# A slot's scores for the maxima in one block, its turned scores in another, with one wait for two banks each

## The chip, the cores and the metric

The kernel runs on one core of a Trainium2 chip. The metric is the device time of one execution in microseconds (us). Before the change it is 510.05 us, the median of three runs (509.32 to 510.07).

## The reference

Two layers act on `x` of shape 16 x 128 x 256 (batch, token, channel). Layer 0 is a WKV recurrence over the 128 tokens and a gated feed-forward with 704 hidden units. Layer 1 is a cross-attention and a mixture of eight experts plus a shared expert. The change lies in the cross-attention alone:

```
q = Wq @ layernorm(x) + bq;  k = Wk @ ctx + bk;  v = Wv @ ctx + bv      # 128 x 256 each
dot  = einsum('bhdt,bhds->bhts', q, k) / sqrt(8)                        # 16 heads of 8 dims
mask = target_mask[..., None] * source_mask[..., None, :]
dot  = mask * dot - (1 - mask) * 1e6
amap = softmax(dot, axis=-1) * mask
out  = einsum('bhts,bhds->bhdt', amap, v)
```

Per batch that is 16 heads of 256 x 256 scores. Sixteen batches are computed one behind the other.

## The kernel before

The kernel is written engine by engine, with semaphores set and waited for by hand; what an engine does, it does in the order in which it is written. In the attention the scores of every head are computed twice on TensorE (PE).

**Scores for the maxima.** `score` (L1190) multiplies a stack of 60 rows (bf16 parts of q, k and the mask) into a 128 x 512 bank of PSUM: two matmuls, tt = 0 and 1, each 128 queries by 256 keys. VectorE (DVE) takes the maximum over the keys of each query straight from the bank (`dve_reduce`, L1325). It does so two batches ahead. The negative maxima are turned (`pe_mxT`, L1279), copied by ScalarE (ACT, L1355), split into parts on GpSimd (POOL) and brought by DMA into the stack, so that the second computation subtracts them.

**Turned scores.** `score_T` (L1205) computes the same head with keys as rows, again two matmuls into one bank. ACT takes the exponential of the bank (`act_exp`, L1374) and writes it to SBUF. Eight matmuls of 32 columns (`pe_pv`, L1291) multiply it with the values and a column of ones, two slots later.

**Halves.** Head 2p and head 2p+1 of the maxima lie in different halves of the 128 rows (0 to 59 and 64 to 123), and so do the two halves of the turned heads. Matmuls in different halves run beside each other: their starts in the trace are 0.003 us apart.

**Slots.** A batch has 8 slots. Slot p of batch b holds, on PE (`pe_both`): scores 2p and 2p+1 for the maxima of batch b+2, turned scores 2p and 2p+1 of batch b, then the value matmuls of slot p-2. In slot 1 the value matmuls (`between`) stand inside `pe_both`, because they end the previous batch, and ACT copies their result (`act_av`, L1381) between its two exponentials of slot 1. Other work of PE follows in certain slots: the transpose of maxima behind slot 0, the four transposes of the previous batch's values (`pe_yT`, L1300) behind slot 3, two more (`pe_yo`, L1307) behind slot 5, a query projection (L688) behind slot 6. DVE's slot holds two maxima, and behind them in slot 3 the reciprocal of the sums (L1333, which waits for the four transposes), in slot 4 two products (L1340), in slot 5 the addition to X (L1348). ACT's slot holds two exponentials, with L1355 behind slot 0, a copy to PARTS (L717) behind slots 2 and 4, and L707 behind slot 7.

**Banks.** Scores for maxima use three banks (`SBK3`), turned scores three others (`TBK3`). Score n uses bank n mod 3, but score 15 uses that of 13 (`THIRDS`, L1167). `last_use(n)` is the score before n that used the same bank: n-3 in general, 13 for 15, 12 of the batch before for 0, and 15 of the batch before for 1. A score waits until maxima `last_use(n)` are taken (`a_red`), a turned one until exponential `last_use(m)` is done (`a_exp`). This order `pe_both` runs in 14 turns, from 179 to 341 us of the span. The first two batches' scores for maxima are written ahead of that, by `pe_scores` (L1230), a pair of heads at a time: head 2p tt 0, head 2p+1 tt 0, head 2p tt 1, head 2p+1 tt 1.

In `pe_both` before, each half of a slot is a group of four matmuls:

```
score_bank(pe, *to_score, n)                # wait: bank of score n
score(pe, to_score[1], n, 0, to)
turned_bank(pe, *to_turn, i, st, half)      # wait: bank of the turned score
score_T(pe, to_turn[1], i, st, 2 * half)
score(pe, to_score[1], n, 1, to).then_inc(a_s, 1)
score_T(pe, to_turn[1], i, st, 2 * half + 1).then_inc(a_st, 1)
```

Of the kernel before, what the change touches and what calls it, by code (L numbers as in the profile page):

```python
# [14 lines left out]
NG, GB = 4, 4  # L15
# [3 lines left out]
HEADS, HD = 16, 8  # L19
# [31 lines left out]
def flamingo_kernel(nc, x, ctx, mask, g_xattn, g_ffn, time_decay, time_first, gate_wT, up_wT, down_wT,  # L51
# [11 lines left out]
    with ExitStack() as keep:  # L63
# [161 lines left out]
        with ExitStack() as part:  # L225
# [8 lines left out]
            def semp(name):  # L234
                return sem(name, part)
# [126 lines left out]
            def later(count):  # L362

                return not isinstance(count, int) or count > 0
# [762 lines left out]
            with ExitStack() as att:  # L1127
# [18 lines left out]
                a_mx = [semp(f"a_mx{k}") for k in range(NS)]  # L1146
# [4 lines left out]
                a_s = semp("a_s")  # L1151
                a_red = semp("a_red")
# [3 lines left out]
                a_st = semp("a_st")  # L1156
                a_exp = semp("a_exp")
# [9 lines left out]
                THIRDS = [n % 3 for n in range(HEADS - 1)] + [1]  # L1167
                SBK3, TBK3 = [bank[2], bank[0], bank[1]], bank[3:6]

                def last_use(n):  # L1170

                    return max(m for m in range(-HEADS, n) if THIRDS[m % HEADS] == THIRDS[n])
# [6 lines left out]
                def rows_of(h):  # L1179

                    lo = 64 * (h // HALF)
                    return slice(lo, lo + STACK), h % HALF

                def head_of(n):

                    return n // 2 + HALF * (n % 2)

                def score(pe, k, n, tt, to):
                    rows, h = rows_of(head_of(n))
                    return pe.matmul(to[:, tt * T:(tt + 1) * T], QKA[rows, k, 0, h, tt * P:(tt + 1) * P],  # L1190
                                     QKA[rows, k, 1, h, :], start=True, stop=True)
# [5 lines left out]
                def turned_head(q, m):  # L1197

                    return HALF * (m // 2) + 2 * column_of(q, m) + q % 2

                def score_T(pe, k, q, st, m, to=None):
                    rows, h = rows_of(turned_head(q, m))
                    if to is None:
                        to = TBK3[THIRDS[turned_at(q, st, m // 2)]]
                    return pe.matmul(to[:, (m % 2) * T:(m % 2 + 1) * T], QKA[rows, k, 1, h, st * P:(st + 1) * P],  # L1205
                                     QKA[rows, k, 0, h, :], start=True, stop=True)

                def turned_at(i, st, half):

                    return 2 * (2 * i + st) + 1 - half  # L1210

                def score_filled(pe, g, k, n):

                    if n == 0:
                        pe.wait_ge(a_qa[k], 32 * (g + 1))

                def score_bank(pe, g, k, n):

                    score_filled(pe, g, k, n)
                    pe.wait_ge(a_red, HEADS * (GB * g + k) + last_use(n) + 1)  # L1220

                def turned_bank(pe, g, k, i, st, half):

                    b, m = GB * g + k, turned_at(i, st, half)
                    if m == 0:
                        pe.wait_ge(a_mx[k], 32 * (g + 1))
                    if later(HEADS * b + last_use(m) + 1):
                        pe.wait_ge(a_exp, HEADS * b + last_use(m) + 1)
# [31 lines left out]
                def pe_both(pe, to_score, to_turn, p, between):  # L1260


                    i, st = p // 2, p % 2
                    for n, half in ((2 * p, 1), (2 * p + 1, 0)):
                        to = SBK3[THIRDS[n]]
                        if first(GB * to_turn[0] + to_turn[1]) and n in (1, 2):
                            pe.wait_ge(s_x2, 1 + 2 * G3 + n)
                        score_bank(pe, *to_score, n)
                        score(pe, to_score[1], n, 0, to)
                        turned_bank(pe, *to_turn, i, st, half)  # L1270
                        score_T(pe, to_turn[1], i, st, 2 * half)
                        score(pe, to_score[1], n, 1, to).then_inc(a_s, 1)
                        score_T(pe, to_turn[1], i, st, 2 * half + 1).then_inc(a_st, 1)
                        if half == 1:
                            between()

                def pe_mxT(pe, g, k):
                    pe.wait_ge(a_red, HEADS * (GB * g + k + 1))
# [180 lines left out]
                def first(b):  # L1459

                    return isinstance(b, int) and b == 0
# [35 lines left out]
                with nc.Block() as block:  # L1497
# [143 lines left out]
                    def _(pe):  # L1641
# [41 lines left out]
                        def slot(_, g, k, p):  # L1683
# [14 lines left out]
                            if there(b, AHEAD_S):  # L1698
                                pe_both(pe, at(g, k, AHEAD_S), (g, k), p, values if p == 1 else nothing)
                            elif there(b):  # L1700
                                pe_scoresT(pe, g, k, i, st)
# [597 lines left out]
```

## Time and profile before

| | |
|---|---|
| median of three runs | 510.05 us |
| the profiled execution | 509.36 us |
| its span, first to last instruction | 507.6 us |
| granted TensorE clock, mean | 0.997 |
| PE busy in the span | 474.1 us (93%) |
| DVE busy | 381.3 us (75%) |
| ACT busy | 244.9 us (48%) |
| POOL busy | 230.1 us (45%) |

The span runs from the first instruction to the last; the execution's time is 1.8 us more. Matmuls are pipelined and overlap, so "busy" of PE says that some matmul was under way, not that the array worked at its peak. A mean of 273 ns for a score matmul is its latency; the next one in the same half starts 0.11 to 0.12 us later. The time an engine sat idle ahead of a group is written behind the group, with the instruction that released it.

### The profile page before, as it was taken

The numbers are of one execution on the slowest core, as the hardware profiler recorded it, in microseconds if no ns is written. First come the engines' busy times: TensorE is split into PE (matmuls) and PEld (weight loads), VectorE is DVE, ScalarE is ACT, GpSimd is POOL, SyncE is SP. The second block draws the span as 40 slices with busy tenths as digits, with TensorE's granted clock in tenths as the row PEclk, the third lists the DMA queues.
The fourth block names the chain that finished last, engine by engine and source line by source line (L and its number), as shares of the span: only waits on it lengthen the run. The fifth ranks groups of instructions, "written<-read, shape, count | busy, mean of one in ns | idle before, by whom it ended". The sixth has DMA issues, their size and how long they took to land. (4 is left out here: it accounts for less than half of the span.)

```text
span 507.6 us, 10286 instructions
## 1 busy us (share of the span) xinstructions
PE 474.1 (93%) x3384; PEld 259.3 (51%) x3384; DVE 381.3 (75%) x765; ACT 244.9 (48%) x461; POOL 230.1 (45%) x319
## 2 busy tenths in 40 slices
PE   2998999998999999999999998998999999999993
PEld 2663664854733633343343333333445647788882
DVE  4989889899888789999999999998465633333321
ACT  2761232332232078889999998787412010233331
POOL 3736434154755355867677763213010660042433
PEclk9999999999999999999999999999999999999998
DMA  7750175002775116566566655300022224378843
GB/s 237 216 176 0 43 166 89 2 0 62 186 195 150 54 57 174 147 171 184 162 163 172 171 153 147 84 5 5 1 94 77 74 94 166 120 185 195 192 112 41
DMA packets 67256, 59.96 MB, mean 118 GB/s; under 512 B 10048, under 2 KB 62256, under 8 KB 67216
## 3 DMA queue, kind: packets, MB, share of 16 engines
q1 hardware_dynamic: 63712, 55.24, 39.6%
q0 software_dynamic: 3072, 4.21, 4.9%
q8 instruction: 22, 0.36, 0.3%
q14 instruction: 18, 0.15, 0.1%
q10 hardware_dynamic: 432, 0.00, 0.0%
HBM read 38.90 MB, written 22.50 MB: 121 GB/s over the span
## 5 line engine op out<-in xcount | busy, mean ns | idle before, releaser
L1325 DVE TENSOR_REDUCE MX<-psum 128x2 f32<-128x512 f32 x256 | 162.1, 682 | 10.0 <-PE psum L1190 8.4
L1374 ACT ACTIVATE HP<-psum 128x512 f32<-128x512 f32 x224 | 122.1, 602 | 28.9 <-PE psum L1205 26.4
L1190 PE MATMUL psum<-QKA 60*128 60x256 bf16 x512 | 81.3, 273 | 7.1 <-DVE MX L1325 5.6
L1205 PE MATMUL psum<-QKA 60*128 60x256 bf16 x512 | 81.1, 273 | 1.5 <-DMA QKA<-max_scr 1.0
L1291 PE MATMUL psum<-HP,VP 128*32 128x256 f32 x1024 | 81.8, 391 | 0.3 <-issue 0.2
L602 PE MATMUL psum<-space_a,space_w 128*128 128x512 f32 x160 | 73.1, 602 | 1.9 <-DVE HP L629 1.9
L1190 PEld LDWEIGHTS psum<-QKA 60*128 60x128 bf16 x512 | 31.6, 94 | 63.8 <-DVE MX L1325 44.6
L1966 POOL DMA_INDIRECT out_x<-OE,to_u x16 | 24.9, 1557 | 62.6 <-ACT OE L2001 60.1
L602 PEld LDWEIGHTS psum<-space_a,space_w 128*128 128x128 f32 x160 | 29.0, 190 | 36.5 <-issue 31.0
L2089 PE MATMUL psum<-XT,WE 128*128 128x256 f32 (+1 forms) x192 | 44.0, 379 | 0.9 <-ACT XT L1985 0.9
L199 PE MATMUL psum<-space_a,wsh 128*128 128x512 f32 (+1 forms) x96 | 43.6, 598 | 0.3 <-PEq L1497 0.3
L615 ACT ACTIVATE space_a<-psum,hgs 128x512 f32<-128x512 f32 (+1 forms) x24 | 15.6, 649 | 54.8 <-PE psum L602 49.5
L2089 PEld LDWEIGHTS psum<-XT,WE 128*128 128x128 f32 (+1 forms) x192 | 34.3, 181 | 7.3 <-issue 1.1
L1291 PEld LDWEIGHTS psum<-HP,VP 128*32 128x32 f32 x1024 | 20.6, 108 | 28.8 <-issue 18.1
L1205 PEld LDWEIGHTS psum<-QKA 60*128 60x128 bf16 x512 | 30.6, 94 | 6.9 <-issue 3.6
L2250 DVE SCALAR_TENSOR_TENSOR KR<-KR,psum 128x256 f32<-128x256 f32 (+1 forms) x24 | 10.1, 420 | 30.0 <-ACT KR L1992 30.0
L1413 POOL TENSOR_TENSOR NP<-NM,zeros 32x128 bf16<-32x128 f32 x32 | 14.3, 446 | 36.6 <-ACT NM L1355 35.3
L644 PE MATMUL psum<-space_w,HP 128*128 128x256 f32 x120 | 27.3, 381 | 0.9 <-PEq L795 0.9
L199 PEld LDWEIGHTS psum<-space_a,wsh 128*128 128x128 f32 (+1 forms) x96 | 16.6, 181 | 21.2 <-issue 21.1
L739 POOL TENSOR_TENSOR QK<-QK,PARTS 128x512 f32<-128x512 f32 x16 | 18.5, 1157 | 18.9 <-ACT PARTS L717 18.8
L489 DVE RECIPROCAL DEN<-DEN 128x256 f32<-128x256 f32 (+1 forms) x12 | 27.0, 2264 | 0.0
L1992 ACT ACTIVATE KR<-psum 128x256 f32<-128x256 f32 (+1 forms) x24 | 9.2, 382 | 36.9 <-PE psum L2089 36.9
(207 smaller groups left out, 767.3 us busy)
## 6 DMA issues: line engine op xcount, KB each, us to landing
QKA<-stack_scr SPq DMA_DIRECT2D x32, 480.0 KB, 4.5
stack_scr<-PARTS SPq DMA_DIRECT2D x32, 192.0 KB, 2.1
WE<-in_W SPq DMA_DIRECT2D x16, 352.0 KB, 4.0
stack_scr<-PARTS SPq DMA_DIRECT2D x32, 128.0 KB, 2.0
XD<-dispatched SPq DMA_DIRECT2D x8, 258.0 KB, 3.9
X<-in_x SPq DMA_DIRECT2D x4, 512.0 KB, 5.8
CTX<-in_ctx SPq DMA_DIRECT2D x4, 512.0 KB, 8.2
MB<-in_mask SPq DMA_DIRECT2D x16, 128.0 KB, 3.3
```

What stands on the lines that cost most here:

```text
L199: last = pe.matmul(bank[2 * i + side][0:m, :], (wsh1, wsh3)[side][:, h, i * P:i * P + m], ZT4[:, h, bass.ds(GT * g, GT)], start=(h == 0), ...
L489: dve.reciprocal(DEN[:, h, x], DEN[:, h, x]).then_inc(s_rec, 1)
L602: last = pe.matmul(to[:, :], w[:, h, i * P:(i + 1) * P], ZT[:, h, :], start=(h == 0), stop=(h == 1))
L644: pe.matmul(to[f], HP[:, i, t * P:(t + 1) * P], dw[:, i, :], start=(i == 0), stop=False)
L739: pool.tensor_tensor(QK2 if r == 0 else part_of(2), QK2, part_of(r), ALU.subtract).then_inc(a_rest, 1)
L1190: return pe.matmul(to[:, tt * T:(tt + 1) * T], QKA[rows, k, 0, h, tt * P:(tt + 1) * P], QKA[rows, k, 1, h, :], start=True, stop=True)
L1205: return pe.matmul(to[:, (m % 2) * T:(m % 2 + 1) * T], QKA[rows, k, 1, h, st * P:(st + 1) * P], QKA[rows, k, 0, h, :], start=True, stop=True)
L1291: last = pe.matmul(PVB[32 * j:32 * j + 32, (m // 2) * T:(m // 2 + 1) * T], VP[:, k, st, turned_head(i, m), :], PT[:, i % 2, st, m, :], sta ...
L1325: dve.tensor_reduce(MX[:, par, head_of(n), :], src[:, :].rearrange("p (a s) -> p a s", a=2), axis=AX.X, op=ALU.max).then_inc(a_red, 1)
L1374: act.activation(PT[:, i % 2, st, 2 * half:2 * half + 2, :].rearrange("p j t -> p (j t)"), TBK3[THIRDS[m]], ACT.Exp).then_inc(a_exp, 1)
L1966: pool.indirect_dma_start(out=out_rows, out_offset=bass.IndirectOffsetOnAxis(ap=to_u[:, e, a:a + 1], axis=0), in_=OE[:, s, a, :], in_offse ...
L2089: last = pe.matmul(bank[i][0:m, lo:lo + CAP], w[:, s, h, i * P:i * P + m], XT[:, s, h, :], start=(h == 0), stop=(h == 1))
```

## The change

In each slot of `pe_both`, the four matmuls of the two scores for the maxima come first, then (in slot 1) the value matmuls, then the four turned ones. Ahead of the first block stands one wait for the maxima of `last_use(2p+1)`, ahead of the second one wait for the exponential of `last_use` of the slot's second turned score. The matmuls are the same in number, operands and banks. A score's semaphore is still raised by its second matmul.

```
-                    for n, half in ((2 * p, 1), (2 * p + 1, 0)):
-                        to = SBK3[THIRDS[n]]
+                    for n in (2 * p, 2 * p + 1):
                         if first(GB * to_turn[0] + to_turn[1]) and n in (1, 2):
                             pe.wait_ge(s_x2, 1 + 2 * G3 + n)
-                        score_bank(pe, *to_score, n)
-                        score(pe, to_score[1], n, 0, to)
-                        turned_bank(pe, *to_turn, i, st, half)
-                        score_T(pe, to_turn[1], i, st, 2 * half)
-                        score(pe, to_score[1], n, 1, to).then_inc(a_s, 1)
-                        score_T(pe, to_turn[1], i, st, 2 * half + 1).then_inc(a_st, 1)
-                        if half == 1:
-                            between()
+                        score_filled(pe, *to_score, n)
+                    pe.wait_ge(a_red, HEADS * (GB * to_score[0] + to_score[1]) + last_use(2 * p + 1) + 1)
+                    for tt in range(2):
+                        for n in (2 * p, 2 * p + 1):
+                            last = score(pe, to_score[1], n, tt, SBK3[THIRDS[n]])
+                            if tt == 1:
+                                last.then_inc(a_s, 1)
+                    between()
+                    if p == 0:
+                        pe.wait_ge(a_mx[to_turn[1]], 32 * (to_turn[0] + 1))
+                    b, m = GB * to_turn[0] + to_turn[1], turned_at(i, st, 0)
+                    if later(HEADS * b + last_use(m) + 1):
+                        pe.wait_ge(a_exp, HEADS * b + last_use(m) + 1)
+                    for j in range(2):
+                        for half in (1, 0):
+                            last = score_T(pe, to_turn[1], i, st, 2 * half + j)
+                            if j == 1:
+                                last.then_inc(a_st, 1)
```

## Rows read from the trace of the kernel before

**Rows 1.** The 14 turns: busy us of PE, PEld, DVE, ACT, POOL; clock, DMA.
```profile
180.30:341.20 160.90, 154.46 (x1879) 60.40 (x1879) 153.92 (x285) 142.14 (x283) 95.62 (x158) 1.00 0.53 141
```

**Rows 2.** Groups from 210 to 300 us: busy, mean ns | idle before, releaser.
```profile
L1325 DVE TENSOR_REDUCE MX<-psum 128x2 f32<-128x512 f32 x125 | 79.5, 683 | 4.0 <-PE psum L1190 3.1
L1374 ACT ACTIVATE HP<-psum 128x512 f32<-128x512 f32 x124 | 67.5, 602 | 8.9 <-PE psum L1205 7.4
```

**Rows 3.** Timeline of DVE: start us, us, instruction, count, idle before it.
```profile
235.00 3.95 DVE L1325 TENSOR_REDUCE MX<-psum 128x2 f32<-128x512 f32 x6
239.15 0.69 DVE L1325 TENSOR_REDUCE MX<-psum 128x2 f32<-128x512 f32 x1 [0.20 <-PE psum L1190]
240.04 3.08 DVE L1325 TENSOR_REDUCE MX<-psum 128x2 f32<-128x512 f32 x5 [0.20 <-PE psum L1190]
243.04 0.34 DVE L1333 RECIPROCAL RD<-psum 128x32 f32<-128x32 f32 x1
243.31 1.28 DVE L1325 TENSOR_REDUCE MX<-psum 128x2 f32<-128x512 f32 x2
244.50 0.60 DVE L1340 SCALAR_TENSOR_TENSOR YA<-psum,maskG,RD 128x128 f32<-128x128 f32 x2
245.02 1.28 DVE L1325 TENSOR_REDUCE MX<-psum 128x2 f32<-128x512 f32 x2
246.21 0.41 DVE L1348 TENSOR_TENSOR X<-X,psum 128x256 f32 x1
246.54 3.94 DVE L1325 TENSOR_REDUCE MX<-psum 128x2 f32<-128x512 f32 x6
...
248.42 0.68 DVE L1325 TENSOR_REDUCE MX<-psum 128x2 f32<-128x512 f32 x1
```

**Rows 4.** Timeline of ACT in the same batch.
```profile
239.26 0.60 ACT L1374 ACTIVATE HP<-psum 128x512 f32<-128x512 f32 x1 [0.17 <-PE psum L1205]
239.75 0.59 ACT L1381 ACTIVATE AV<-psum 128x512 f32<-128x512 f32 x1
...
240.72 0.60 ACT L1374 ACTIVATE HP<-psum 128x512 f32<-128x512 f32 x1
241.67 0.65 ACT L717 ACTIVATE PARTS<-QK 128x512 bf16<-128x512 f32 x1
242.19 2.30 ACT L1374 ACTIVATE HP<-psum 128x512 f32<-128x512 f32 x4
```

**Rows 5.** Timeline of PE in the same batch.
```profile
238.50 0.28 PE L1279 MATMUL psum<-ident,MX 128*32 128x128 f32 x1
238.72 0.28 PE L1190 MATMUL psum<-QKA 60*128 60x256 bf16 x1
238.72 0.28 PE L1205 MATMUL psum<-QKA 60*128 60x256 bf16 x1
...
239.04 0.64 PE L1291 MATMUL psum<-HP,VP 128*32 128x256 f32 x8
239.62 0.28 PE L1190 MATMUL psum<-QKA 60*128 60x256 bf16 x1
...
239.85 0.27 PE L1190 MATMUL psum<-QKA 60*128 60x256 bf16 x1
...
241.39 0.28 PE L1205 MATMUL psum<-QKA 60*128 60x256 bf16 x1
...
242.28 0.66 PE L1300 MATMUL psum<-ident,AV 128*128 128x128 f32 x4
242.87 0.28 PE L1190 MATMUL psum<-QKA 60*128 60x256 bf16 x1
...
249.16 0.28 PE L1190 MATMUL psum<-QKA 60*128 60x256 bf16 x1
```

**Rows 6.** Timelines of PE and DVE in the prologue, around one pair.
```profile
165.07 0.39 PE L1190 MATMUL psum<-QKA 60*128 60x256 bf16 x4 [0.79 <-DVE MX L1325]
165.48 0.69 DVE L1325 TENSOR_REDUCE MX<-psum 128x2 f32<-128x512 f32 x1
```

## The prediction

> **What bounds the kernel now.** I read the share of busy time first. Over the 160.90 us in which both kinds of scores are written, PE is busy for 154.46 us, DVE for 153.92 and ACT for 142.14 [rows 1]. No engine is far from full, so any wait that the change puts between two of them has little room to vanish in. The groups of instructions show who waits: in 90 us DVE waits 4.0 us ahead of 125 maxima and ACT 8.9 us ahead of 124 exponentials, nearly all of it for PE [rows 2]. 125 maxima in 90 us are 11.52 us for a batch of 16. The timeline of DVE shows the same period (the batch's third last pair starts at 235.00 and at 246.54, 11.54 us apart) and where the waits stand: 0.20 us ahead of the maxima of score 2 (239.15) and of score 3 (240.04), and about 0.2 us ahead of score 0, inside the merged line at 235.00 [rows 3]. Last I read the chain PE -> DVE -> PE for its latencies, since the change only moves matmuls and waits: it removes no instruction that computes.
>
> **Constants, each read from a row.** Within a batch I count from the first score matmul, S0 = 0. S, T, V are the starts of a slot's score matmuls, turned-score matmuls and value matmuls; R(n) and E(n) the starts of reduction n and exponential n.
> - Reductions back to back: (3.08 - 0.68) / 4 = 0.60 apart. The reciprocal adds 0.27 (243.04 to 243.31), the two products 0.52 (244.50 to 245.02), the addition to X 0.33 (246.21 to 246.54) [rows 3].
> - A bank given back: the reduction at 248.42 ends 0.68 later, at 249.10, and the score that needs the bank starts at 249.16 [rows 3, 5]. So S >= R(n) + 0.74.
> - Scores to reduction: S at 238.72, R at 239.15: 0.43 [rows 3, 5]. Four matmuls of two heads written as a pair stand in the prologue already: 0.39 us from first start to last end, then R at 165.48, 0.41 after the start [rows 6]. So a pair costs no more time than one head did, because the heads of a pair lie in different halves of the rows, and R(2p) >= S + 0.43.
> - Turned scores to exponential: T 238.72, E 239.26: 0.54. Exponentials are 0.49 apart (239.26 to 239.75), the copy AV takes 0.49, a PARTS copy 0.52 (241.67 to 242.19) [rows 4, 5].
> - Turned bank given back: E at 240.72 ends 0.60 later, T starts at 241.39. So T >= E(n) + 0.67 [rows 4, 5]; I use 0.66.
> - PE in order: S to V 0.32 (238.72 to 239.04), V to the next 0.58 (239.04 to 239.62; I use 0.57), two matmul pairs 0.23 (239.62 to 239.85), the transpose of the maxima 0.22 (238.50 to 238.72), the four of AV 0.59 (242.28 to 242.87) [rows 5].
>
> **What the change does to each slot.** A slot now waits once, for the later of the banks of its two scores, writes the four score matmuls, waits once for the later of the two turned banks, and writes the four turned ones. The same matmuls overlap two by two as before, so the matmul time is unchanged at zero difference (0.39 us for four shows it [rows 6]). Each slot has two waits on PE fewer. No row prices a wait that is already met; two such steps stand inside the 0.23 us from 239.62 to 239.85, two matmul pairs that take 2 x 0.11 [rows 5], so they are worth between 0 and 0.01 us, and I take 0. What remains is what each wait holds back.
>
> *Middle slots (p = 1 to 6)* wait for the maxima of score 2p-2: R(2p) >= R(2p-2) + 0.74 + 0.43 = 1.17, against two reductions, 1.20. It fits with 0.03 to spare, if PE is there on time.
> *Slots 7 and 0.* Score 15 has the bank of 13, and score 1 of the next batch the bank of 15. Now score 14 waits for maxima 13 and score 0 for maxima 15, the one just ahead. R(14) - R(13) and R(0) - R(15) become 1.17 instead of 0.60: 0.57 of idle DVE twice, where now about 0.06 and 0.2 stand.
> *Slot 1.* The value matmuls (between) stand between the scores and both turned scores. That is good for the reductions: R(2) = S1 + 0.43 and R(3) follows 0.60 later, so the waits of 0.20 there go. But T1 comes after V, 0.9 us later than S1, and what is queued behind it on ACT is the exponential, then AV, then the other exponential.
>
> Walk through one batch: S0 0, R0 0.43, R1 1.03, T0 0.22, E0 0.76, E1 1.25, V 0.54, maxima's transpose 1.11 (0.57 after V), S1 1.33, R2 1.76, R3 2.36. V of slot 1 at 1.65, T1 2.22, E2 2.76, AV 3.25, E3 3.74. S2 = R2 + 0.74 = 2.50, R4 2.96, R5 3.56. T2 needs E2's bank: 2.76 + 0.66 = 3.42 (without that wait it would be 2.73). V 3.74, S3 4.31: R6 is 4.74, where DVE was ready at 4.16, 0.58 lost. E4 4.23, T3 = 4.23 + 0.66 = 4.89, V 5.21, the transposes of AV 5.78, S4 6.37. The reciprocal waits for those transposes (0.66 long, plus 0.04): 6.48, where R7 + 0.60 = 5.94: 0.54 lost again. R8 = S4 + 0.43 = 6.80. From here DVE leads: S5 7.54; R9 7.40, the products 8.00, R10 8.52, R11 9.12, addition 9.72, R12 10.05, R13 10.65, S7 = 11.39, R14 11.82, R15 12.42, and S0 of the next batch at 13.16. ACT is ready for it: E15 = T7 + 0.54 + 0.49 = 12.64, its bank is free at 13.30, T0 would start at 13.38.
>
> The period is 13.16 us. In check: 16 x 0.60 = 9.60, operations between 1.12, waits 0.57 + 0.57 + 0.13 (R2) + 0.58 + 0.54 + 0.05 (R8) = 2.44.
>
> **The sum.** 14 turns run in this order. The first has no AV, transposes of values or reciprocal behind it; the walk without them gives about 11.3. Twelve take 13.16, and the last, up to the end of its reduction 15, 12.42 - 0.43 + 0.68 = 12.67. Together 11.3 + 157.9 + 12.7 = 181.9, against 160.9 [rows 1]: +21.0 us. The profiled execution took 509.36 us (span 507.6), 0.14% below the median of 510.05; 509.36 + 21.0 = 530.4, and I say 530.5. Nothing before or behind this stretch is changed, and the stretch ends on PE and DVE together, so its delay reaches the end in full.
>
> What no row shows is how ACT behaves once the turned scores wait for its exponentials in pairs. Low bound: T2 and T3 cost nothing, and only slots 7 and 0 and R2 count: 9.60 + 1.12 + 0.57 + 0.57 + 0.13 = 11.99, 0.47 above 11.52, some 14 x 0.47 = +6.6, 516. High bound: the loss of slot 3 occurs once more, in slot 4 (0.4 a batch, +5.6), 536. The rows stand nearest to the walk, whose waits of T are all longer than 0.3 us past what PE would reach by itself.
>
> The Trainium skill, "TensorE: Matmul & The Clock Gate", Part 3, "The cost: per-tile semaphore tail", says that increments which concurrent matmuls make on completion serialise, about 26 ns each. The change puts two such increments side by side. The prologue's pair has them side by side too, and its reduction starts 0.02 us after the pair's last modelled end, against 0.03 to 0.04 with one head [rows 3, 5, 6]: the trace does not show the cost. By the rule, an estimate with 26 ns in each of the five places where a pair leads straight into a wait is 0.13 a batch, 1.8 us, 532.
>
> **The rivals.**
> (a) *ACT's wait is hidden, only the ends of a batch cost*: 516, as worked out. For it: ACT has 18.8 us of idle in the stretch [rows 1]. Against it: that idle is 1.3 us a batch, and the order exp, AV, exp in slot 1 cannot use it before E2.
> (b) *Faster.* The reductions 2 and 3 lose their waits of 0.20 each in the middle of the batch [rows 3], and the waits at the batch's ends cost nothing. Price: 0.4 x 14 = 5.6 us, 504. It decides if a bank comes back early enough, within 0.60 - 0.43 = 0.17 us of the start of a reduction, or if PE is so late at slots 7 and 0 anyway that the wait is over. The rows have 0.74 for the first, and for the second only 0.2 of lateness.
> (c) *No change*: the gain of (b) and some 0.4 a batch at the ends cancel: 510. It needs T2 hidden as well.
> (d) *Worse*: ACT's lateness is not recovered by slot 5 but carried into the next batch, 0.5 to 1 us more a batch: 537 to 545. For it: ACT has 1.3 us of slack a batch and the walk takes most of it in slots 1 to 4. Against it: in slots 5 to 7 the walk has PE wait for DVE, not ACT.
>
> **How the numbers follow.** Forecast 0.76, with its own range 524 to 535; (a) 0.10; (d) 0.08; (b) 0.03; (c) 0.03. What can be told from no change here is about 0.2%. Slower is the forecast, (a) and (d), 0.94; same is (c), 0.03; faster (b), 0.03. The range for 8 times in 10 is 520 to 536.
>
> **What would show it.** In the trace after: a period of about 13.2 us; DVE idle of 0.5 to 0.6 us ahead of maxima 14, 0 and 6 and ahead of the reciprocal, none ahead of maxima 3; the turned scores of slot 2 about 0.9 us after its scores, not with them; PE waiting for ACT where now it waits for DVE alone. Wrong would be: a period under 12.2 (then ACT's wait was hidden), turned scores of slot 2 right behind their scores, or reductions 14 and 0 at 0.60 from the ones ahead.

## The result and the profile after

The changed kernel takes 530.19 us, the median of five runs (529.57 to 530.97), beside 510.05 us before: a ratio of 1.040, 95% interval 1.0385 to 1.0414. It is 20.1 us slower; 530.5 was forecast. In the profiled execution the span grew from 507.6 to 527.8 us.

All of it lies in the 14 turns. The busy time of each engine in the same stretch as in [rows 1], and in the rest of the span behind it:

```profile
180.20:362.00 181.80, 153.75 (x1887) 60.42 (x1891) 157.16 (x287) 140.93 (x284) 95.40 (x158) 1.00 0.47 125
```
```profile
361.40:527.80 166.40, 154.97 (x793) 101.97 (x793) 73.70 (x204) 46.69 (x82) 48.57 (x50) 0.99 0.40 104
```

From the first reduction of the first turn (180.25) to the end of the last (361.34) it is 181.1 us, against 160.9. What follows takes 166.4 us, as it did before. PE, DVE and ACT do the same work; the time is idle time on all three at once. (DVE's busy time reads 3.2 us more: the window reaches 0.7 us past the turns, and two reductions back to back share 0.08 us that a waited-for one doesn't.) The groups from 230 to 320 us show who waits, as in [rows 2]:

```profile
L1334 DVE TENSOR_REDUCE MX<-psum 128x2 f32<-128x512 f32 x111 | 70.8, 685 | 12.1 <-PE psum L1190 11.9
L1383 ACT ACTIVATE HP<-psum 128x512 f32<-128x512 f32 x111 | 60.6, 606 | 18.0 <-PE psum L1205 18.0
L1300 PE MATMUL psum<-HP,VP 128*32 128x256 f32 x440 | 35.1, 391 | 1.8 <-ACT AV L1390 1.7
L1190 PE MATMUL psum<-QKA 60*128 60x256 bf16 x220 | 21.6, 274 | 7.3 <-DVE MX L1334 7.3
L1205 PE MATMUL psum<-QKA 60*128 60x256 bf16 x220 | 21.2, 271 | 3.3 <-ACT HP L1383 3.3
```

DVE's idle time ahead of the maxima was 4.0 us in 90 and is 12.1; ACT's was 8.9 and is 18.0. PE itself had stood idle for only 0.8 us ahead of score matmuls and not at all ahead of turned ones and values (210 to 300 us of the kernel before); now it is 7.3, 3.3 and 1.8. (Lines behind L1276 of the kernel are 9 further down than before.)

One whole batch on DVE, as in [rows 3]. Its period is 13.11 us, from 256.90 to 270.01:

```profile
256.90 3.81 DVE L1334 TENSOR_REDUCE MX<-psum 128x2 f32<-128x512 f32 x6 [0.48 <-PE psum L1190]
261.52 1.29 DVE L1334 TENSOR_REDUCE MX<-psum 128x2 f32<-128x512 f32 x2 [0.80 <-PE psum L1190]
262.90 0.36 DVE L1342 RECIPROCAL RD<-psum 128x32 f32<-128x32 f32 x1
263.23 1.29 DVE L1334 TENSOR_REDUCE MX<-psum 128x2 f32<-128x512 f32 x2
264.43 0.60 DVE L1349 SCALAR_TENSOR_TENSOR YA<-psum,maskG,RD 128x128 f32<-128x128 f32 x2
264.95 1.28 DVE L1334 TENSOR_REDUCE MX<-psum 128x2 f32<-128x512 f32 x2
266.14 0.41 DVE L1357 TENSOR_TENSOR X<-X,psum 128x256 f32 x1
266.47 1.28 DVE L1334 TENSOR_REDUCE MX<-psum 128x2 f32<-128x512 f32 x2
268.24 1.29 DVE L1334 TENSOR_REDUCE MX<-psum 128x2 f32<-128x512 f32 x2 [0.48 <-PE psum L1190]
270.01 1.29 DVE L1334 TENSOR_REDUCE MX<-psum 128x2 f32<-128x512 f32 x2 [0.48 <-PE psum L1190]
```

The reader sees three holes: ahead of maxima 6 (261.52), of 14 (268.24) and of 0 (270.01). The row of maxima 0 is the same wait as at 256.90. A reduction is 0.68 long and the next one starts 0.60 behind its start, so a printed idle of 0.48 costs 0.57: from 266.47 + 0.60 = 267.07, maxima 13, to 268.24 is 1.17. The waits ahead of maxima 2 and 3 have shrunk to 0.13 us together, so that all six from 256.90 on stand in one line (3.81, where six back to back take 5 x 0.60 + 0.68 = 3.68).

Counted in this way, from start to start, the 1.55 us by which a steady batch grew (11.56 to 13.11) are: maxima 0, a wait of 0.56 for 0.19; maxima 14, 0.57 for 0.07; maxima 6, 0.89 for none; the reciprocal, 0.18 for none, and 0.05 behind it; less 0.44 at maxima 2 and 3 (0.12 and 0.01, for 0.28 and 0.29).

PE in the first half of that batch, as in [rows 5]:

```profile
256.48 0.39 PE L1190 MATMUL psum<-QKA 60*128 60x256 bf16 x4 [0.59 <-DVE MX L1334]
256.70 0.38 PE L1205 MATMUL psum<-QKA 60*128 60x256 bf16 x4
257.02 0.64 PE L1300 MATMUL psum<-HP,VP 128*32 128x256 f32 x8
257.59 0.28 PE L1288 MATMUL psum<-ident,MX 128*32 128x128 f32 x1
257.80 0.39 PE L1190 MATMUL psum<-QKA 60*128 60x256 bf16 x4
258.12 0.64 PE L1300 MATMUL psum<-HP,VP 128*32 128x256 f32 x8
258.69 0.39 PE L1205 MATMUL psum<-QKA 60*128 60x256 bf16 x4
258.98 0.39 PE L1190 MATMUL psum<-QKA 60*128 60x256 bf16 x4
259.85 0.39 PE L1205 MATMUL psum<-QKA 60*128 60x256 bf16 x4 [0.48 <-ACT HP L1383]
260.52 0.64 PE L1300 MATMUL psum<-HP,VP 128*32 128x256 f32 x8 [0.28 <-ACT AV L1390]
261.09 0.39 PE L1190 MATMUL psum<-QKA 60*128 60x256 bf16 x4
```

and ACT beside it, as in [rows 4]:

```profile
259.20 0.60 ACT L1383 ACTIVATE HP<-psum 128x512 f32<-128x512 f32 x1 [0.77 <-PE psum L1205]
259.69 0.59 ACT L1390 ACTIVATE AV<-psum 128x512 f32<-128x512 f32 x1
```

Read in order: the scores of slot 1 start at 257.80, the value matmuls at 258.12, and only then, at 258.69, the turned scores. ACT, idle for 0.77 us, gets its exponential at 259.20. The turned scores of slot 2 wait until it has ended (259.80) and start at 259.85, 0.87 us behind their scores. The value matmuls wait once more, for AV, and PE comes to slot 3 at 261.09.

### The profile page after: what moved, and what is told of

The parts are those of the page before. It is cut to its first block and busy times, and to the rows that moved or that the text cites. A ratio compares the mean times of both kernels' runs of the same rounds, so it can differ in the third digit from the quotient of the medians.

```text
span 527.8 us, 10250 instructions
## 1 busy us (share of the span) xinstructions
PE 472.7 (90%) x3384; PEld 258.9 (49%) x3384; DVE 384.0 (73%) x765; ACT 243.3 (46%) x461; POOL 229.9 (44%) x319
## 3 DMA queue, kind: packets, MB, share of 16 engines
q0 software_dynamic: 3072, 4.21, 4.7%
## 5 line engine op out<-in xcount | busy, mean ns | idle before, releaser
L1190 PE MATMUL psum<-QKA 60*128 60x256 bf16 x512 | 50.6, 274 | 19.7 <-DVE MX L1334 19.6
L1205 PE MATMUL psum<-QKA 60*128 60x256 bf16 x512 | 49.7, 271 | 7.8 <-ACT HP L1383 5.9
L1190 PEld LDWEIGHTS psum<-QKA 60*128 60x128 bf16 x512 | 15.0, 94 | 63.5 <-DVE MX L1334 52.1
L1422 POOL TENSOR_TENSOR NP<-NM,zeros 32x128 bf16<-32x128 f32 x32 | 14.2, 444 | 43.4 <-ACT NM L1364 42.1
L1205 PEld LDWEIGHTS psum<-QKA 60*128 60x128 bf16 x512 | 19.9, 94 | 26.1 <-ACT HP L1383 14.3
```

## The experiments

Twelve kernels ran. "Period" is the mean over six batches in the middle (maxima 0 of the sixth to maxima 0 of the twelfth), read from the profiled execution. The kernel before ran again beside each group of them (medians of 509.3 to 509.6 us); the ratio is to those runs, with a 95% interval of 0.002 or less to either side.

| kernel | built on | time us | ratio | period us |
|---|---|---|---|---|
| before | | 510.05 | 1 | 11.56 |
| changed | | 530.19 | 1.040 | 13.11 |
| e1 first turned score ahead, own waits for turned | changed | 523.07 | 1.027 | 12.47 |
| e2 own waits for scores in slots 7, 0 | changed | 527.77 | 1.036 | 13.03 |
| e3 values last in slot 1 | changed | 523.05 | 1.028 | 12.47 |
| e4 AV ahead of both exponentials | changed | 528.54 | 1.036 | 12.93 |
| e5 own waits for turned scores | changed | 531.48 | 1.044 | 13.12 |
| e6 all own waits | changed | 526.96 | 1.035 | 12.98 |
| e7 merged score wait | before | 526.34 | 1.033 | 12.65 |
| e8 values last in slot 1 | before | 511.57 | 1.005 | 11.73 |
| e9 e1 + e2 | changed | 519.71 | 1.019 | 12.33 |
| e10 e3 + e2 | changed | 521.02 | 1.023 | 12.38 |
| e11 score 15 in the bank of 12 | changed | 524.65 | 1.030 | 12.74 |
| e12 transpose of maxima behind slot 1 | before | 508.51 | 0.998 | 11.57 |

The theory: two chains cost. One is DVE -> PE -> DVE at the ends of a batch, where the merged wait is for the reduction just ahead. The other is PE -> ACT -> PE in slots 1 to 3, which starts because the order puts the first turned score of slot 1 behind the value matmuls. The rivals: the merged waits cost and the order is free; or the costs are separate and add up.

**e1, e3: the order in slot 1.** e1 puts the first turned score ahead of the values, e3 both:

```
...
+                    for half in (1, 0):                               # e1
+                        turned_bank(pe, *to_turn, i, st, half)
+                        score_T(pe, to_turn[1], i, st, 2 * half)
+                        score_T(pe, to_turn[1], i, st, 2 * half + 1).then_inc(a_st, 1)
+                        if half == 1:
+                            between()
```
```
-                    between()                                         # e3
...
                             if j == 1:
                                 last.then_inc(a_st, 1)
+                    between()
```

> The changed kernel, but each turned score has its own wait again, and the first of a slot stands ahead of the value matmuls of slot 1. Theory (order): of the 20 us, the part from slot 1 to slot 3 goes, because the exponential of slot 1 no longer waits behind the value matmuls; the 0.57 us of idle DVE ahead of maxima 14 and 0 stay. The two turned scores overlap less well (0.11 us more a slot). Period 12.7 us against 13.11, about 525 us. Rival (every cost but the batch's ends came from the turned side): period 12.0, 516 us. Rival (only the wait for two score banks costs, the order is free): unchanged at 530.

> The changed kernel, but in slot 1 the value matmuls come behind the turned scores instead of ahead of them; all waits stay as changed. Theory (order): turned scores of slot 1 start 0.6 us earlier, the exponential and the copy AV too, the loss ahead of maxima 6 falls from 0.9 to about 0.3 us; period 12.5 us, about 522 us. Rival (the waits for two banks cost, not the order): 530.

Both came to 523 us, 7 us below the changed kernel (expected 525 and 522), with 12.47 us a batch for 12.7 and 12.5. DVE in e1:

```profile
253.66 5.19 DVE L1329 TENSOR_REDUCE MX<-psum 128x2 f32<-128x512 f32 x8 [0.48 <-PE psum L1190]
259.07 0.36 DVE L1337 RECIPROCAL RD<-psum 128x32 f32<-128x32 f32 x1 [0.22 <-PE psum L1304]
```

The hole ahead of maxima 6 is gone: eight maxima in one line. One of 0.30 us stands ahead of the reciprocal instead of 0.18. In e3 the hole ahead of maxima 6 is 0.25 and the other stays at 0.18. e3 differs from the changed kernel in nothing but the place of the value matmuls; it keeps the merged wait on the turned side and gains as much as e1, which undoes it, so the order is the cost and not that wait. The wait ahead of maxima 0 stays in both.

**e5, e6: waits undone, order kept.** e5 takes e1's loop with `between()` ahead of it; e6 also gives each score its own wait:

```
+                    for n in (2 * p, 2 * p + 1):                      # e6
+                        pe.wait_ge(a_red, ... + last_use(n) + 1)
+                        score(pe, to_score[1], n, 0, SBK3[THIRDS[n]])
+                        score(pe, to_score[1], n, 1, SBK3[THIRDS[n]]).then_inc(a_s, 1)
...
```

> The changed kernel with its order, but each turned score again has its own wait. Theory (order): the second turned score of slot 2 waits for the exponential of slot 1 in either form, so only the wait's merging is undone and that costs nothing: within 2 us of 530, period 13.0 to 13.1. Rival (the merged wait on the turned side costs): the turned scores start up to 0.5 us earlier a slot, 520 to 523 us.

> The new order (two scores, values, two turned scores) with all four waits of before, each at its own bank. Theory (order): as with own waits in slots 7 and 0 alone, period about 12.7 us, 525 us: most of the 20 us is the order's. Rival (the merged waits are the whole cost): 510, as before.

531.5 and 527.0 (the theory had 525 for e6). With every merged wait undone the kernel is still 3.5% slower than before. That alone doesn't fell the first rival, because e6 also writes one score's two matmuls behind the other's, where the changed kernel alternates them. The rival falls by two pairs that differ only in the place of the value matmuls: e1 beside e5 (523.1 for 531.5) and e3 beside the changed kernel (523.1 for 530.2). In e5 the second turned score of slot 2 still waits for the exponential of slot 1:

```profile
259.19 0.38 PE L1205 MATMUL psum<-QKA 60*128 60x256 bf16 x2
259.84 0.39 PE L1205 MATMUL psum<-QKA 60*128 60x256 bf16 x2 [0.27 <-ACT HP L1377]
```

**e2, e7, e11: the ends of a batch.** e2 gives slots 7 and 0 own waits. e7 adds only the merged score wait to the kernel before. e11 lets score 15 have the bank of 12 (turned scores unchanged), so that slot 7 waits for maxima 12, while slot 0 waits for 15 as it did:

```
+                        if half == 1:                                 # e7, in before
+                            pe.wait_ge(a_red, ... + last_use(2 * p + 1) + 1)
...
```
```
+                S_BANK = [n % 3 for n in range(HEADS)]                # e11
...
-                    pe.wait_ge(a_red, ... + last_use(2 * p + 1) + 1)
+                    pe.wait_ge(a_red, ... + max(last_score(2 * p), last_score(2 * p + 1)) + 1)
```

> The changed kernel, but in slots 7 and 0 each of the two scores has its own wait and is written on its own. Theory (order, a coupled chain): the wait ahead of maxima 14 and 0 goes, but PE comes late for both by itself (it leaves the projection 0.36 us after maxima 13 begin), so only 0.4 us of the 1.1 come back: period 12.7 us, about 525 us, with 0.2 us of idle ahead of maxima 14, 0.3 ahead of 0 and 0.4 ahead of 2. Rival (costs add up): 2 x 0.57 less, period 12.0, 515 to 516 us.

> The order of the kernel before, but the wait for both score banks stands ahead of a slot's first score; the turned scores keep their own waits. Theory: maxima 14 and 0 start 1.17 us after the ones ahead, nothing else changes, and since DVE is then what PE waits for, both count nearly in full: period 12.3 to 12.5 us, 520 to 523 us. Rival (PE was late there anyway): at most 0.3 a batch, 513 or less.

> The changed kernel, but score 15 takes the bank of 12 instead of 13; score 0 of the next batch then takes the bank of 15, so slot 0 waits for maxima 15 as it did. Only slot 7's wait moves, from maxima 13 to 12. Theory: PE comes to slot 7 about 0.36 us after maxima 13 begin, so maxima 14 start 0.8 us after 13 instead of 1.17, and the rest of the chain is shifted by it in full: period 12.7 to 12.75 us, 525 us. Rival (as in the kernel with own waits at the ends, nearly nothing comes back): 529.

e11 came out as expected, 524.65 for 525: moving one wait by one reduction returns 5.5 us, 0.37 a batch, nearly all of the 0.39 by which its hole shrank. DVE in e11, maxima 12 to 15 in one line of 2.67 (a hole of 0.18 ahead of 14 instead of 0.57) and the hole ahead of 0 as before:

```profile
251.90 2.67 DVE L1339 TENSOR_REDUCE MX<-psum 128x2 f32<-128x512 f32 x4
255.06 0.69 DVE L1339 TENSOR_REDUCE MX<-psum 128x2 f32<-128x512 f32 x1 [0.48 <-PE psum L1195]
```

e2 returned 2.4 us where adding up would give 14 to 15 and I expected 5. Both holes shrink, from 0.57 and 0.56 to 0.18 and 0.29, but a new one opens ahead of maxima 2 (printed idle 0.57, a wait of 0.66 for 0.12). PE and DVE in e2:

```profile
255.32 0.67 PE L1190 MATMUL psum<-QKA 60*128 60x256 bf16 x4
256.08 0.39 PE L1205 MATMUL psum<-QKA 60*128 60x256 bf16 x4
256.40 0.64 PE L1306 MATMUL psum<-HP,VP 128*32 128x256 f32 x8
256.97 0.28 PE L1294 MATMUL psum<-ident,MX 128*32 128x128 f32 x1
257.19 0.39 PE L1190 MATMUL psum<-QKA 60*128 60x256 bf16 x4
...
257.62 1.29 DVE L1340 TENSOR_REDUCE MX<-psum 128x2 f32<-128x512 f32 x2 [0.57 <-PE psum L1190]
```

The scores of slot 0 start early (255.32), but the turned pair behind them waits until 256.08 for exponential 15, and slot 1 is at 257.19, 1.87 us behind slot 0 instead of 1.32. I had left that wait out of e2's expectation. Not all of the 0.55 is that wait: with a wait of its own for each score, the four take 0.67 us instead of 0.39. In e9 (below), where each turned score has its own wait too, the first one starts 0.51 behind the scores, against 0.22 in the changed kernel and 0.76 here. So e2 puts a cost of its own in the place of the one that it takes away, and its 2.4 us are not the price of the merged wait.

e7 took 526.3, beyond the 520 to 523 expected. The ends cost what they should (maxima 0 0.57 for 0.19, maxima 14 0.56 for 0.07), but the period of 12.65 us is above 12.3 to 12.5, because the reciprocal now starts 0.23 us late as well: 260.27, where 257.04 + 5 x 0.60 = 260.04 was due.

```profile
257.04 3.08 DVE L1327 TENSOR_REDUCE MX<-psum 128x2 f32<-128x512 f32 x5 [0.20 <-PE psum L1190]
260.27 0.36 DVE L1335 RECIPROCAL RD<-psum 128x32 f32<-128x32 f32 x1
```

And two of its batches took 14.2 and 14.1 us. Of these the last section tells.

**e4: the wait for AV.** `between()` on ACT moves ahead of both exponentials of slot 1.

```
+                    between()
                     for half in (1, 0):
...
-                        if half == 1:
-                            between()
```

> The changed kernel, but on ACT the copy AV comes ahead of both exponentials of slot 1, not between them. The value matmuls of slot 2 wait for that copy in the changed kernel (they start 0.84 us after it starts). Theory: the copy then runs in ACT's idle time before the first turned score of slot 1 is ready, the value matmuls of slot 2 start as soon as the turned scores are issued, and the loss ahead of maxima 6 falls by 0.2 to 0.3 us, some of which comes back at the reciprocal: period 12.95 us, about 528 us. Rival (slot 2 is late only because of its turned scores' wait): unchanged at 530.

528.5, period 12.93, as expected. PE no longer waits for AV, so that wait is real. The 0.2 us a batch are the net of two things, though: exponential 2 now stands behind the copy, and the turned scores of slot 2 start 3.57 us behind S0 instead of 3.37.

**e9, e10: both repairs.**

> The changed kernel with both repairs: own waits in slots 7 and 0 for the scores, own waits for all turned scores, and the first turned score of slot 1 ahead of the value matmuls. Theory (coupled chain): the ends' wait still returns only 0.1 to 0.2 us a batch, since PE is late there; period 12.3 us, 519 to 521 us. Rival (costs add up): 523 less 2 x 0.57 x 14 = 507, not slower than before.

> The changed kernel with the value matmuls of slot 1 last and own waits for the scores of slots 7 and 0; turned scores keep their merged wait. Theory: 0.1 to 0.2 us a batch below the one with the values last alone, period 12.3 us, 520 to 521 us, and turned scores of slot 0 wait for exponential 15. Rival (costs add up): 507 to 508.

519.7 and 521.0, at the forecast and some 13 us above the rival's sum. What the edits return does add up: 0.64 (e3) and 0.08 (e2) a batch are 0.72, and e10 returned 0.73. e9 has the waits of the kernel before except in slots 1 to 6, where two scores share one, and its two scores, and its two turned scores, stand together. It is still 1.9% slower. PE in slot 0, first the kernel before, then e9:

```profile
237.24 0.28 PE L1190 MATMUL psum<-QKA 60*128 60x256 bf16 x1
237.24 0.28 PE L1205 MATMUL psum<-QKA 60*128 60x256 bf16 x1
...
237.94 0.64 PE L1291 MATMUL psum<-HP,VP 128*32 128x256 f32 x8
```
```profile
253.10 0.67 PE L1190 MATMUL psum<-QKA 60*128 60x256 bf16 x4
253.61 0.63 PE L1205 MATMUL psum<-QKA 60*128 60x256 bf16 x4
254.18 0.64 PE L1301 MATMUL psum<-HP,VP 128*32 128x256 f32 x8
```

Before, the value matmuls start 0.70 us behind the first score, in e9 1.08. In the order before, a score runs beside a turned score and both waits are passed with the same matmuls. In e9 the two scores stand apart because their waits do, with no turned score to fill the other half of the rows, and the turned ones wait behind the second: the second score starts at 253.38, 0.05 us behind the end of maxima 15, and the second turned score at 253.86, 0.05 behind the end of the last exponential of the batch before. In slot 4 of the same batch, where nothing holds PE up, the four turned scores, with the same two waits, take 0.38 us; in slot 0 they take 0.63.

**e8, e12: can the kernel before be bettered?** e8 moves the values of slot 1 behind both halves of the slot. e12 moves the transpose of the maxima (`p == 0` to `p == 1` on PE, and its copy on ACT).

> The kernel before, but the value matmuls of slot 1 behind both halves of the slot instead of between them. Theory: the wait of 0.29 us ahead of maxima 3 goes, but the copy AV comes 0.2 us later and with it the value matmuls of slot 2, and the wait reappears ahead of maxima 6: within 0.3% of 510. Rival (the middle waits can be gained): 4 us less, 506.

> The kernel before, with the transpose of the maxima (PE) and its copy (ACT) behind slot 1 instead of behind slot 0. PE then comes to score 2 0.22 us earlier. Theory: the waits ahead of maxima 2 and 3 shrink by 0.2 us, but the four transposes of AV and the reciprocal are no earlier, so the wait reappears ahead of the reciprocal or maxima 8: within 0.3% of before. Rival (DVE is the bound and PE's lateness is the only loss): 3 us less, 506 to 507.

e8: 511.6, 0.5% slower (0.34 to 0.68%), a little outside the 0.3% expected. The hole ahead of maxima 3 goes. Of what comes back, 0.11 us is ahead of maxima 6, where I expected it all, and 0.31 ahead of the reciprocal:

```profile
251.13 3.80 DVE L1324 TENSOR_REDUCE MX<-psum 128x2 f32<-128x512 f32 x6 [0.20 <-PE psum L1190]
255.17 0.36 DVE L1332 RECIPROCAL RD<-psum 128x32 f32<-128x32 f32 x1 [0.23 <-PE psum L1299]
```

e12: 508.5 against 509.4 of the kernel before in the same set, ratio 0.9979 (0.9971 to 0.9988). It is faster than the kernel before by 0.2%, at the edge of what is told apart here. Its mean period in the middle, 11.57, looks like that of before, but one batch of the six took 12.28 us and the others 11.37 to 11.52 (before: 11.46 to 11.69). In that batch score 0 waited for the transfer that brings the stack:

```profile
237.27 0.28 PE L1190 MATMUL psum<-QKA 60*128 60x256 bf16 x1 [0.83 <-DMA QKA<-stack_scr]
```

So the gain of about 0.1 us a batch is in the steady batches. The wait ahead of maxima 2, 0.28 before, is 0 to 0.07; that ahead of maxima 3 stays, and 0.05 stand ahead of the reciprocal. Whether the wait for the transfer comes from the edit is open; no such batch stands in the profile of the kernel before.

## Why the prediction was right

*The sum.* Forecast 11.3 + 12 x 13.16 + 12.67 = 181.9 us for the turns; measured 11.2 (first turn), 13.11 in the steady turns, 12.5 (last), 181.1 in all.

*Ends of a batch.* R(14) - R(13) = 1.17 was forecast and is 1.17; R(0) - R(15) is 1.16 for 1.17. For maxima 14 the reason is shown by e11, which moves that wait alone; no run moves the wait ahead of maxima 0 alone, and e7 shows both together.

*Slot 1.* Measured from the first score, the walk had S1 1.33, T1 2.22, T2 3.42, S4 6.37; the trace has 1.32, 2.21, 3.37, 6.32. e3, and e1 beside e5, show that the place of the values is the cause.

*Slots 2 and 3, mis-sized.* The walk let the value matmuls of slot 2 start at 3.74. They start at 4.04, because `pe_pv` waits there for AV. That term was missed. The hole ahead of maxima 6 is therefore 0.89 us (1.49 for 0.60), not 0.58, and the one ahead of the reciprocal 0.18 (262.90, where 262.72 was due), not 0.54. So two of the signs that were named, 0.5 to 0.6 ahead of maxima 6 and ahead of the reciprocal, did not come true one by one; both sums are 1.1. That is not luck alone: the walk already held T3 back until E4's bank came free. T3 starts at 4.84 for 4.89, and there both waits end at once: 0.23 behind S3, and 0.06 behind the end of E4 (261.26). So PE's wait for AV ran beside work of ACT that was counted, the slot's values came at 5.16 for 5.21, and everything behind is set by PE from there. e4, which moves AV, returns 0.2 us a batch net.

*Rival (a), the wait of ACT hidden, 516:* fallen by the changed kernel itself. *Rival (b) and (c):* the waits ahead of maxima 2 and 3 did shrink, as they said, and the time came back ahead of 6. Their price was too low: a printed idle of 0.20 costs 0.28, so (b) should have read 0.57 a batch and about 8 us, not 5.6. *Rival (d), lateness carried over:* did not occur; the period stays at 13.11, and PE waits for DVE ahead of slot 6 (0.16 us) and slot 7 (0.32), as argued. *The increments side by side:* no trace of a cost; R0 starts 0.42 us behind S0 here (256.48 to 256.90), 0.43 with one head [rows 3, 5]. But the comparison is weaker than the prediction took it to be: in the kernel before, the last matmuls of a score and of a turned score raise their semaphores 3 ns apart too (239.735 and 239.739), so the change adds no such pair, and R0 waits for the first of the two increments only.

What the prediction did not see is how little of the ends' cost can be had back in this order by waits alone. Added to the kernel before, the merged score wait costs 12.65 - 11.56 = 1.1 us a batch (e7). In the changed kernel own waits at the ends return 0.08 (e2), since they bring the cost described there; moving the bank for one of the two places, which leaves the matmuls alone, returns 0.37 (e11).

## What to carry to other kernels

One wait for two buffers waits for the later one. Count, for every place in the rotation and above all where it wraps, how far back that buffer's reader stands: two readers back was free here (1.17 us of round trip against 1.20 of work), one back cost 0.57 (1.17 against 0.60). Where a wait must come earlier, try another bank before splitting the block: e11 returned 5.5 us, e2 2.4. Before a block is moved behind another on one engine, look at what is queued behind its consumer, and work the chain through one period from measured latencies; the price lay two slots further on. And don't read the gain of a repair from the hole it fills, unless it leaves the rest as it is: with three engines within 12% of full, the next wait stands right behind (e2, e8).

## What the runs showed of the hardware

Two things I had not expected. TensorE's clock fell in a kernel whose PE waits more. In e7, of these stretches (columns as in [rows 1]), the second and the fifth had a granted clock of 0.57 and 0.59, near the lower of its two levels (1.2 of 2.4 GHz):

```profile
312.00:318.00 6.00, 4.21 (x57) 1.90 (x56) 4.96 (x10) 3.93 (x8) 2.61 (x4) 1.00 0.73 209
318.00:322.00 4.00, 4.00 (x39) 1.30 (x34) 2.20 (x4) 2.68 (x6) 1.73 (x5) 0.57 0.56 140
322.00:326.00 4.00, 3.64 (x49) 1.51 (x46) 3.93 (x8) 3.19 (x7) 1.44 (x3) 1.00 0.44 111
326.00:332.00 6.00, 4.21 (x56) 1.88 (x57) 5.06 (x10) 3.62 (x7) 0.00 (x0) 0.99 0.08 18
332.00:336.00 4.00, 4.00 (x38) 1.39 (x36) 2.06 (x4) 2.31 (x5) 1.31 (x3) 0.59 0.53 127
```

Ahead of either fall PE was busy for 4.21 of 6 us. The batches with it took 14.2 and 14.1 us, 1.4 to 1.5 more than the others, about 3 us in all; without them e7 would stand at about 523 (an estimate), the edge of what was expected. How much PE waited does not explain the fall by itself. In the changed kernel it was busy for less, and the clock stayed at 1.00:

```profile
319.35:325.35 6.00, 4.07 (x53) 1.56 (x53) 4.89 (x9) 3.41 (x9) 1.95 (x6) 1.00 0.69 197
```

What set it off in e7 is open. In the profiled execution of the changed kernel the clock was 1.00 throughout the turns, so it has no part in the 20 us. In the profiled executions of e3, e4, e9 and e10 it was 0.79 from 180 to 188 us. Their first turns took 12.5, 12.5, 11.8 and 11.8 us, against 11.2 in the changed kernel and 10.5 in e2, which has the score waits of e9 and e10. So some 1.3 us of their times may be the clock's, and e9 without it would still be 1.6% slower than before (an estimate).

The other is how soon a matmul follows ACT. A turned score (bf16) starts 0.05 us after the exponential that frees its bank has ended (259.20 + 0.60 to 259.85). The value matmuls (f32), released by AV, start 0.24 us after it (259.69 + 0.59 to 260.52). Their weight load is not what fills the 0.24: in the trace the first one starts at 260.51, 0.01 ahead of the first matmul. What does is open.
